# One transposing transfer for both halves of the probabilities, and the fourth query tile finished in its own slot

## The reference, cut to what matters

```
x = layernorm(x + self_attention_0(x))        # causal, rotary embedding on q and k
x = layernorm(x + cross_attention_0(x, ctx))  # RMS norm on q and k
x = layernorm(x + ffn_0(x))                   # 4 experts, silu
x = layernorm(x + self_attention_1(x))        # causal
x = layernorm(x + cross_attention_1(x, ctx))  # grouped heads, mask
x = layernorm(x + ffn_1(x))                   # quantised to fp8 steps
```

```
q, k, v = heads(x @ Wq), heads(x @ Wk), heads(x @ Wv)     # self0: q, k = rope(q), rope(k)
p   = softmax(where(causal, q @ k.T * scale, -inf))
out = (p @ v) in heads, then @ Wo
```

## Time and profile before

| | |
|---|---|
| median of 3 runs | 2684.7 us (2680.32 to 2685.36) |
| profiled execution | 2686.01 us, span 2684.1 us |
| busy: PE, DVE, ACT, POOL | 2436.8, 1852.3, 1587.0, 715.6 us |
| mean granted TensorE clock | 0.964 of 2.4 GHz |
| transposing transfers in the attentions | 512 of the high, 512 of the low half |

### The profile page before, as it was taken

One profiled execution on the slowest core, in us unless ns is written; L12 is line 12 of the kernel. 1 busy time (PEld: TensorE's weight loads), 2 busy tenths in 40 slices (PEclk: granted clock), 3 DMA queues, 4 the chain that ended last, 5 costly groups with the idle time before them and its releaser, 6 DMA issues. The chain is left out here.

```text
span 2684.1 us, 58413 instructions
## 1 busy us (share of the span) xinstructions
PE 2436.8 (91%) x21345; PEld 1575.8 (59%) x21584; DVE 1852.3 (69%) x3371; ACT 1587.0 (59%) x2718; POOL 715.6 (27%) x671
## 2 busy tenths in 40 slices
PE   6988997989999999999678999998899999999964
PEld 4555664546666666665355666665466666665432
DVE  4776676657777777775556666667478888885597
ACT  4767665158877778874134555554167777774243
POOL 5565656601111011112233222215300000012211
PEclk8999999999999999999888999999899999999987
DMA  3333335325666666666240334435167777776400
GB/s 91 87 75 84 85 73 106 118 48 108 114 116 116 109 111 116 114 112 131 106 165 3 97 86 90 92 84 136 36 123 144 145 145 145 148 150 131 108 0 32
DMA packets 777604, 273.63 MB, mean 102 GB/s; under 512 B 746097, under 2 KB 748913, under 8 KB 775793
## 3 DMA queue, kind: packets, MB, share of 16 engines
q1 hardware_dynamic: 775696, 265.85, 47.0%
q0 software_dynamic: 1760, 5.77, 0.9%
HBM read 84.55 MB, written 6.44 MB: 34 GB/s over the span
## 5 line engine op out<-in xcount | busy, mean ns | idle before, releaser
L846 ACT ACTIVATE ph<-p,ri 128x1024 bf16<-128x1024 f32 (+4 forms) x512 | 437.4, 854 | 455.7 <-DVE ri L1155 367.7
L1165 DVE SCALAR_TENSOR_TENSOR pl<-p,ri,ph 128x1024 bf16<-128x1024 f32 (+4 forms) x512 | 510.5, 997 | 141.0 <-issue 71.7
L1225 PE MATMUL ps<-wo_hi,v_hi 128*128 128x128 bf16 x2688 | 479.2, 220 | 65.8 <-DMA wo_lo<-pl 65.2
L1227 PE MATMUL ps<-wo_hi,v_lo 128*128 128x128 bf16 x2688 | 478.9, 220 | 0.0
L1226 PE MATMUL ps<-wo_lo,v_hi 128*128 128x128 bf16 x2688 | 478.8, 220 | 0.0
L857 ACT ACTIVATE p<-p,nb 128x1024 f32<-128x1024 f32 (+4 forms) x512 | 435.5, 851 | 49.6 <-DVE nb L1148 36.3
L1225 PEld LDWEIGHTS ps<-wo_hi,v_hi 128*128 128x128 bf16 x2688 | 263.6, 98 | 139.4 <-DMA wo_lo<-pl 91.0
L1226 PEld LDWEIGHTS ps<-wo_lo,v_hi 128*128 128x128 bf16 x2688 | 263.9, 98 | 37.4
L1226 PE MATMUL ps<-k_lo,q_hi 128*128 128x512 bf16 (+2 forms) x767 | 271.5, 354 | 7.1 <-issue 0.4
L1227 PE MATMUL ps<-k_hi,q_lo 128*128 128x512 bf16 (+3 forms) x768 | 271.7, 354 | 0.1
L1227 PEld LDWEIGHTS ps<-wo_hi,v_lo 128*128 128x128 bf16 x2688 | 264.1, 98 | 0.0
(11 more groups left out here) (191 smaller groups left out, 5668.9 us busy)
## 6 DMA issues: line engine op xcount, KB each, us to landing
raw_kv<-in_wkvself SPq DMA_DIRECT2D x32, 512.0 KB, 3.6
raw_q<-in_wqself SPq DMA_DIRECT2D x32, 256.0 KB, 2.7
wo_hi<-ph SPq DMA_TRANSPOSE x512, 3.2
wo_lo<-pl SPq DMA_TRANSPOSE x512, 3.1
raw_q<-in_woself SPq DMA_DIRECT2D x32, 256.0 KB, 3.0
raw_q<-in_wqcross SPq DMA_DIRECT2D x32, 256.0 KB, 2.9
raw_q<-in_wocross SPq DMA_DIRECT2D x32, 256.0 KB, 3.0
raw_kv<-in_wkvcross SPq DMA_DIRECT2D x24, 256.0 KB, 3.1
```

Source lines behind the costliest of these rows:

```text
L846: nc.scalar.activation(m["ph"][:, qt % 2, 0:w], m["p"][:, qt % 2, 0:w], ACT.Copy, scale=ri[:, qt % 2:qt % 2 + 1]).then_inc(p_norm, 1)
L1165: nc.vector.scalar_tensor_tensor(out=m["pl"][:, qt % 2, 0:w], in0=m["p"][:, qt % 2, 0:w], scalar=ri[:, qt % 2:qt % 2 + 1], in1=m["ph"][:, ...
L1225: nc.tensor.matmul(o, l(0), r(0), start=first, stop=False)
L1227: return nc.tensor.matmul(o, l(1), r(0), start=False, stop=last)
```

## The change

For the two causal layers:

- `ph` and `pl` of a tile now lie side by side in one tile `phl`, the high half in columns 0 to w and the low half in w to 2w. SP issues one transposing transfer of 2w columns, after the remainder is written, and `tr_in` counts 16 for a tile in place of 32.
- The turned halves of a tile lie behind one another, tiles 0 and 1 in `wo_hi` and tiles 2 and 3 in `wo_lo`.
- ACT's `rounded` and DVE's `inverse` and `remainder` of the fourth tile stand in slot 3 of their own unit, behind that tile's exp and ahead of the V job's copies.
- SP loads a head of the next pair in slot 1 of units with `n % 4` of 0 and 2, behind the transfer of tile 0.
- In self0 POOL's split begins in slot 0 (wkv), ahead of the rotation of q, with wq in slot 1 behind the rotation of k.

For all layers that loop, self0, self1 and cross1, `units` writes four units out, loops six times over four, and writes the last four out.

The diff:

```diff
--- before.py
+++ after.py
@@ -96,3 +96,3 @@
             if n % 4 in (1, 3):
-                first = 1 if self.rope else 2
+                first = 0 if self.rope else 2
                 return n % 4 // 2, {first: [("kv", 0), ("kv", 1)], first + 1: [("q", 0), ("q", 1)]}.get(qt, [])
@@ -218,2 +218,8 @@
 
+        def landed(L, n):
+
+            return c_tr[L.name] + (16 if L.causal else 32) * (n + 1)
+
+        c_tr = dict(self0=0, cross0=16 * UNITS, self1=48 * UNITS, cross1=64 * UNITS)
+
         def units(engine, unit, L):
@@ -224,7 +230,8 @@
                 return
-            unit(0, None)
-            with engine.Fori(0, 7) as it:
+            for n in range(4):
+                unit(n, None)
+            with engine.Fori(0, 6) as it:
                 for i in range(4):
-                    unit(1 + i, it)
-            for n in range(UNITS - 3, UNITS):
+                    unit(4 + i, it)
+            for n in range(UNITS - 4, UNITS):
                 unit(n, None)
@@ -302,7 +309,17 @@
                 m["any"] = sb("any", [P, B], F32, s)
-            m["ph"] = sb(f"ph{li}", [P, 2, L.kv], BF16, s)
-            m["pl"] = sb(f"pl{li}", [P, 2, L.kv], BF16, s)
+            both = sb(f"phl{li}", [P, 4, L.kv], BF16, s)
+            if L.causal:
+                m["phl"] = both[:, :, :].rearrange("p (s k) n -> p s (k n)", s=2)
+                m["ph"] = lambda qt, w, q=m["phl"]: q[:, qt % 2, 0:w]
+                m["pl"] = lambda qt, w, q=m["phl"]: q[:, qt % 2, w:2 * w]
+            else:
+                m["ph"] = lambda qt, w, q=both: q[:, qt % 2, 0:w]
+                m["pl"] = lambda qt, w, q=both: q[:, 2 + qt % 2, 0:w]
             m["wo"] = [sb(f"wo{li}_{k}", [P, H, D], BF16, s) for k in hl]
             tail = [t[:, H // 2:, :].rearrange("p h n -> p (h n)") for t in m["wo"]]
-            m["pT"] = [t[:, 0:QT * L.kt * P].rearrange("p (i k q) -> p i k q", i=QT, k=L.kt) for t in tail]
+            if L.causal:
+                pairs = [t[:, 0:QT * L.kt * P].rearrange("p (i k q) -> p i k q", i=2, k=2 * L.kt) for t in tail]
+                m["pT"] = [pairs[i // 2][:, i % 2, :, :] for i in range(QT)]
+            else:
+                m["pT"] = [t[:, 0:QT * L.kt * P].rearrange("p (i k q) -> p i k q", i=QT, k=L.kt) for t in tail]
             if L.causal:
@@ -441,15 +458,23 @@
                         sp.nop(nofuse=True)
+                    if L.causal:
+                        sp.wait_ge(p_lo, at(count, n, it))
+                        sp.nop(nofuse=True)
+                        sp.dma_start_transpose(m["pT"][qt][:, 0:2 * w // P, :], m["phl"][:, qt % 2, 0:2 * w]).then_inc(tr_in[qt], 16)
+                        return
                     sp.wait_ge(p_norm, at(count, n, it))
                     sp.nop(nofuse=True)
-                    sp.dma_start_transpose(m["pT"][0][:, qt, 0:w // P, :], m["ph"][:, qt % 2, 0:w]).then_inc(tr_in[qt], 16)
+                    sp.dma_start_transpose(m["pT"][0][:, qt, 0:w // P, :], m["ph"](qt, w)).then_inc(tr_in[qt], 16)
                     sp.wait_ge(p_lo, at(count, n, it))
                     sp.nop(nofuse=True)
-                    sp.dma_start_transpose(m["pT"][1][:, qt, 0:w // P, :], m["pl"][:, qt % 2, 0:w]).then_inc(tr_in[qt], 16)
+                    sp.dma_start_transpose(m["pT"][1][:, qt, 0:w // P, :], m["pl"](qt, w)).then_inc(tr_in[qt], 16)
 
                 def unit(n, it):
-                    if n % 4 in (1, 2) and n // 4 < H // 2 - 1:
-                        j = n % 4 - 1
+                    def next_pair():
+                        j = n % 4 // 2 if L.causal else n % 4 - 1
                         sp.wait_ge(w_split, at(lambda n: base + 2 * (n // 4) + j + 1, n, it))
-                        pair = at(lambda n: n // 4 + 1, n, it)
-                        qkv(pair, j, None)
+                        qkv(at(lambda n: n // 4 + 1, n, it), j, None)
+
+                    loading = n % 4 in ((0, 2) if L.causal else (1, 2)) and n // 4 < H // 2 - 1
+                    if loading and not L.causal:
+                        next_pair()
                     if n == UNITS - 3:
@@ -460,2 +485,4 @@
                             transposed(*((n, it, qt - 1) if qt else (n - 1, it, QT - 1)))
+                        if loading and L.causal and qt == 1:
+                            next_pair()
                         k = QT * (n - UNITS + 3) + qt - 2
@@ -643,3 +670,3 @@
                     for qt in range(QT):
-                        if L.rope:
+                        if L.rope and qt:
                             rope(n, it, qt, L.jobs(n, qt))
@@ -654,2 +681,4 @@
                             qkv_piece(L, kind, j, part, at(lambda n: c["whi"] + qkv_item(L, kind, j, n // 4 + 1), n, it))
+                        if L.rope and qt == 0:
+                            rope(n, it, qt, L.jobs(n, qt))
                         k = QT * (n - UNITS + 3) + qt - 1
@@ -843,5 +872,5 @@
                     if bn >= 0:
-                        act.wait_ge(tr_in[bq], at(lambda n: 32 * (c["u"] + behind(n, qt, 2)[0] + 1), n, it))
+                        act.wait_ge(tr_in[bq], at(lambda n: landed(L, behind(n, qt, 2)[0]), n, it))
                     act.wait_ge(r_inv, at(lambda n: c["s"] + QT * n + qt + 1, n, it))
-                    nc.scalar.activation(m["ph"][:, qt % 2, 0:w], m["p"][:, qt % 2, 0:w], ACT.Copy, scale=ri[:, qt % 2:qt % 2 + 1]).then_inc(p_norm, 1)
+                    nc.scalar.activation(m["ph"](qt, w), m["p"][:, qt % 2, 0:w], ACT.Copy, scale=ri[:, qt % 2:qt % 2 + 1]).then_inc(p_norm, 1)
 
@@ -849,3 +878,3 @@
                     for qt in range(QT):
-                        if n or qt:
+                        if qt or n and not (L.causal):
                             rounded(*((n, it, qt - 1) if qt else (n - 1, it, QT - 1)))
@@ -859,2 +888,4 @@
                             rotated(n - 1, it, 1)
+                        if (L.causal) and qt == QT - 1:
+                            rounded(n, it, qt)
                         job_parts(n, it, qt, L.jobs(n, qt))
@@ -879,3 +910,4 @@
                 units(act, unit, L)
-                rounded(UNITS - 1, None, QT - 1)
+                if not (L.causal):
+                    rounded(UNITS - 1, None, QT - 1)
                 if L.name in EARLY:
@@ -1161,7 +1193,7 @@
                     if bn >= 0:
-                        dve.wait_ge(tr_in[bq], at(lambda n: 32 * (c["u"] + behind(n, qt, 2)[0] + 1), n, it))
+                        dve.wait_ge(tr_in[bq], at(lambda n: landed(L, behind(n, qt, 2)[0]), n, it))
                     dve.wait_ge(p_norm, at(lambda n: c["s"] + QT * n + qt + 1, n, it))
                     dve.nop(nofuse=True)
-                    nc.vector.scalar_tensor_tensor(out=m["pl"][:, qt % 2, 0:w], in0=m["p"][:, qt % 2, 0:w], scalar=ri[:, qt % 2:qt % 2 + 1],
-                                                   in1=m["ph"][:, qt % 2, 0:w], op0=ALU.mult, op1=ALU.subtract).then_inc(p_lo, 1)
+                    nc.vector.scalar_tensor_tensor(out=m["pl"](qt, w), in0=m["p"][:, qt % 2, 0:w], scalar=ri[:, qt % 2:qt % 2 + 1],
+                                                   in1=m["ph"](qt, w), op0=ALU.mult, op1=ALU.subtract).then_inc(p_lo, 1)
 
@@ -1170,3 +1202,4 @@
                         prior = (n, it, qt - 1) if qt else (n - 1, it, QT - 1)
-                        if n or qt:
+                        pending = qt or n and not (L.causal)
+                        if pending:
                             inverse(*prior)
@@ -1174,4 +1207,7 @@
                         job_parts(n, it, qt, L.jobs(n, qt), ("QN",))
-                        if n or qt:
+                        if pending:
                             remainder(*prior)
+                        if (L.causal) and qt == QT - 1:
+                            inverse(n, it, qt)
+                            remainder(n, it, qt)
                         if L.rope and qt == 0:
@@ -1199,4 +1235,5 @@
                 units(dve, unit, L)
-                inverse(UNITS - 1, None, QT - 1)
-                remainder(UNITS - 1, None, QT - 1)
+                if not (L.causal):
+                    inverse(UNITS - 1, None, QT - 1)
+                    remainder(UNITS - 1, None, QT - 1)
                 quantise_run(EARLY.get(L.name, ()))
@@ -1368,6 +1405,7 @@
                         pe.wait_ge(o_lo, at(lambda n: CREDIT + c["u"] + n - 1, n, it))
-                    pe.wait_ge(tr_in[qt], at(lambda n: 32 * (c["u"] + n + 1), n, it))
+                    pe.wait_ge(tr_in[qt], at(lambda n: landed(L, n), n, it))
                     v, blocks = L.kvslot(n), L.width(qt) // P
+                    turned_p = (lambda k, kt: m["pT"][qt][:, k * blocks + kt, :]) if L.causal else (lambda k, kt: m["pT"][k][:, qt, kt, :])
                     for kt in range(blocks):
-                        last = three(ps[:, O_BANK + n % 2, qt * P:qt * P + P], lambda k: m["v"][k][:, v, kt, :], lambda k: m["pT"][k][:, qt, kt, :], kt == 0, kt == blocks - 1)
```

(1 more changed line is left out.)

## The result

The changed kernel is slower: 2751.56 us (median of 4 runs, 2743.95 to 2757.51) against 2683.4 us (4 runs of the kernel before beside it), a ratio of 1.0254 with a 95% interval of 1.0228 to 1.028. The profiled execution took 2755.28 us, its span 2753.5 us. The forecast was 2708, and its range ended at 2728. The direction was right, the size was not: +68 us in place of +24.

A forecast was written before the change was run, and what follows sets the result against it. The ACT-DVE-ACT loop was taken to bound self0, PE self1. Self0 +28.8, self1 -2.2 and the ends -2.6 summed to +24 us, giving 2708.7, forecast as 2708; its own range 2698 to 2718, the 8-in-10 range 2678 to 2728.

The forecast's parts named there:

- landing: Fourth tile's ph must wait until tile 1's transfer lands at T+2.56, as it writes the buffer that tile was turned from.
- hold: POOL's wkv_lo stops DVE's fourth remainder until it ends; up to 1.5 us more in a unit with a split.
- the bound of 13.38: Lower bound of a self0 unit: tile 1's transfer never late, loop grows by 0.63 us only, +9.6 us in all.
- I take little of it, since by the same clock wkv_lo has nearly ended when the remainder comes in self0.: In self0 POOL delaying the fourth remainder was bounded at 22 us, 1.5 x 15, and mostly left out.
- at nothing: Mid-unit loads and POOL's earlier split in self0: off the loop, no gain beside the 9.3 us of disturbed units.
- POOL holds the fourth remainder: Rival: in self0 too the split meets the remainder every second unit, +20 us, 2728; chance 0.13.
- T: The end of tile 1's remainder on DVE, from which times within a unit are counted.
- The bounds are 0 and 2.8 us per such unit, and I take 1.4, the middle.: Self1's 14 units with a load: ph up to 1.26 us later, then its remainder up to 1.5 more in wkv_lo.
- the 2.6 us: End of each self attention: the last tile goes one issue (1.29 us) earlier, -2.6 us together.
- The lower clock: Rival: PE's longer waits for v_lo lower its clock; if K's swap is 1 us late every unit, 2738; chance 0.08.
- The landing hidden: Rival: self0's loop grows by 0.63 only (+9.6), self1 loses most idle time (-17), about 2675; chance 0.11.
- SP the bound of self0: Rival: SP and the transfers bound the kernel, so PE's 48.6 us of waits would go, about 2615; chance 0.04.

The follow-up runs named there:

- The short split: The changed kernel with POOL's low halves of wkv and wq cut to 64 columns for all pairs but the first; 2701.88 us, ratio 1.0076.
- the load a slot earlier: The changed kernel with SP's weight loads in slot 0 in place of slot 1, all of POOL's work kept; 2697.0 us, ratio 1.0056.
- the own buffer: The changed kernel with a separate buffer for tile 1's halves, so the fourth ph waits for no transfer of its own unit; 2692.05 us, ratio 1.0037.
- the last experiment: The kernel before with only the fourth tile's reciprocal moved to slot 3, ahead of v_lo; 2682.4 us, ratio 1.0004.
- the kernel with both causes away: The changed kernel with a separate buffer for tile 1's halves and POOL's low halves cut to 64 columns after the first pair; 2663.72 us, ratio 0.993.

## Why the prediction was right or wrong

**What bounds self0: right.** The period of a unit without a load was forecast as 14.02 and is mostly 14.04 to 14.14, with `ph` and exp within 0.1 us of their forecast places. The two terms were then taken off one by one. Without landing and hold the period is 13.43 to 13.53, the bound of 13.38 within 0.15. With the remainder behind the scores again it is 12.75 to 12.86.

**The step that failed in self0: "I take little of it, since by the same clock wkv_lo has nearly ended when the remainder comes in self0."** That timing was before's, where the load is under way early and POOL splits right behind its rotation. The change moves the load to slot 1, so POOL waits for its landing (1.46 us in the long unit above) and wkv_lo meets the fourth remainder in thirteen of the thirty units. By their rows these remainders take 1.70 to 2.44 us in place of 0.75 and lose 14.8 us together, within the 22 that I had as the bound. The short split takes 15.7 us away from self0, the load a slot earlier 14.0. The loads themselves were costed "at nothing", as off the loop; they aren't on it, but they set when POOL starts. The rival "POOL holds the fourth remainder" was the case that came, and its condition (wkv_lo still runs at T+3.3) was met: in the long unit T is 283.13, and wkv_lo ran from T+2.50 to T+4.63.

**The step that failed in self1: "The bounds are 0 and 2.8 us per such unit, and I take 1.4, the middle."** The two costs are not independent, to be averaged. A late landing moves the remainder into wkv_lo, so the second cost comes with the first. Measured in the unit shown: `ph` at T+3.33 (T = 1753.23) where an undisturbed landing gives T+2.6, so 0.7; the remainder 2.55 - 0.75 = 1.8; together 2.5, and the period is 13.95 against the 11.15 forecast for one without a load. Removing the landing removes the link: the own buffer takes 43.4 us off self1, where landing alone, at 0.7 in 14 units, was worth 10. I had taken the hold's bound, 1.5, from a remainder of 256 columns that began 0.41 us into wkv_lo; the one shown begins 0.13 us into it and so loses more. In the window thirteen units have a held remainder. They take 14.22 us in the mean, 3.2 above PE's 11.03, so even the bound of 2.8 was too small. The cause of the rest of these 3.2 us, 0.3 in the unit shown, no run settles.

**The sum.** self0 15.5 us above its term and self1 27.3 above its own. The last units did give more than the 2.6 us, 3.3 and 3.4, but the stretches next to the layers took as much back, so the term comes out as nothing. That makes 45.4, the difference between the +69.4 of the span and the forecast's +24.

**The lower clock.** The granted clock fell as that rival said, 0.97 to 0.94 in self0 and 0.99 to 0.96 in self1, but not in every unit. Here are two units of self0 and two of self1, each from one oT_lo to the next, with the columns of the earlier trace rows:

```profile
230.44:244.57 14.13, 13.03 (x114) 8.10 (x114) 9.55 (x23) 9.24 (x20) 7.28 (x6) 0.88 0.24 46
259.72:273.76 14.04, 11.83 (x114) 7.51 (x114) 9.44 (x23) 9.13 (x20) 7.34 (x6) 1.00 0.24 47
...
1659.32:1670.03 10.71, 10.58 (x107) 7.20 (x108) 6.95 (x21) 6.58 (x16) 1.16 (x1) 1.00 0.31 61
1684.14:1695.96 11.82, 11.68 (x103) 7.37 (x104) 6.92 (x22) 6.80 (x16) 1.16 (x1) 0.86 0.28 55
```

In self0 a short unit takes the same time at 0.88 as at 1.00, though PE is busy 1.2 us longer: the loop hides it. Only two units, at 0.79 and 0.80, are some 0.5 us longer. In self1, where PE is the bound, the unit at 0.86 is 1.1 us longer. Six units without a load run at 0.85 to 0.87 there and take 11.60 to 13.03 us where those at 1.00 take mostly 10.71 to 10.83. Over six times 10.72 that is 7.9 us. So the rival, which I had placed in self0, came in self1. PE's busy time there rose by 13.5 us, and with it the floor of 11.03 a unit that my sum stood on. It falls back to 330.6 in the kernel with the own buffer, where all but the last unit of self1 have a clock of 1.00.

**The landing hidden** (the rival on the faster side) failed by rows: T+2.67. Nor was SP the bound of self0, though the transfers stood nearer than I had them, as the last experiment shows.

## What to carry to other kernels

Find the loop of hand-overs first (who starts as who ends, over one period) and price each moved instruction by whether it stands on it: 0.7 us of remainder moved onto it cost 19.7 us in self0 (401.8 against 382.1), where halving the transfers gave 21.7 in both layers together, and a reciprocal of 0.15 us moved off it gave 14.5. In the whole kernel that remainder costs less, 2663.72 against 2655.97 us: self1 and the last units give some of it back, and the kernel with both causes away also leaves part of POOL's work out. When two costs share a trigger, don't average them; write down when each comes in the changed order, the loads that were moved too, and decide if they meet. And before shortening a loop, look at which supply stands right behind it.

## What the runs showed of the hardware

POOL's subtraction of two SBUF operands stops a DVE scalar_tensor_tensor over SBUF until it has ended: 0.75 us became 1.70, 2.45 and 2.55, and each of them, as the other held ones of these runs, ends 0.54 to 0.56 us after POOL's end. This is an exclusive lock as the Trainium skill has it ("Trainium Architecture — The Big Picture", section "What this means for kernel authors"). The traces agree with that, and also show that the first to start keeps its pace. Where the remainder came 0.31 us ahead it took 0.77 us, and wkv_lo behind it 2.44 in place of 2.13.

POOL's first part, wkv_hi, reads one SBUF operand and stops it as well. With the own buffer the remainder that began 0.34 us into wkv_hi took 1.24 us and ended 0.54 us after it. In the long unit of self0 the remainder of 384 columns came first, took 0.62 us, and wkv_hi took 1.16 in place of 1.04. A DVE subtraction with one operand in PSUM isn't stopped: v_lo took 0.68 us inside wkv_lo, in the kernel with the loads in slot 0.

A transposing transfer of 512 columns issued 1.07 us after a load of 512 KB took 3.30 us from the start of its issue to the release, against 2.48 for the same width without one. Issued 2.64 us after the load, as in the long unit of self0, it took 2.49.
